# A two-layer vision tower on one core: exchanged operand roles in the tokenizer's products, and quantised input rows made three tiles ahead in the last feed-forward stage

## The reference, cut to what matters

```python
# tokenizer: x is [8, 256 features, 64 states, 2 (re, im)], all in fp32
dt = exp(log_dt);  A = -exp(inv_A_real) + 1j * A_imag;  dtA = A * dt[:, None]
dA = (1 + dtA / 2) / (1 - dtA / 2)
V = exp(log(dA)[:, :, None] * arange(256))            # powers 0..255
K = 2 * einsum('chn,hnl->chl', C * B, V).real         # tokens [8, 256, 256]
...
# last network, after a LayerNorm without gain or bias
def fp4_quant_dequant(x):          # blocks of 16 along the last axis
    scale = maximum(max(abs(xb)) / 6, 1e-12)
    return GRID[searchsorted(MID, abs(xb / scale))] * sign(xb) * scale
def fp4_linear(x, w): return quant(x) @ quant(w).T
h = h + fp4_linear(silu(fp4_linear(x, w_gate)) * fp4_linear(x, w_up), w_down)   # 256 -> 704 -> 256
```

## Time and profile before

| | us |
|---|---|
| median of three runs | 1653.43 (1650.32 to 1655.53) |
| the profiled execution | 1650.09 |
| span of its trace | 1648.4 |
| first product of the tokenizer to its last transpose | 55.9 to 117.6 |
| first gate product of the quantised stage to the end of the last residual sum | 1434.6 to 1646.6 |

### The profile page before, as it was taken

How to read it: one execution, slowest core, us unless ns; L and a number is a source line. 1 busy time by engine, 2 the same in 40 slices (tenths; PEclk the granted TensorE clock), 3 DMA queues, 4 the chain that set the end, 5 groups by cost and what they waited for, 6 DMA issues and landing times. The chain is left out here.

```text
span 1648.4 us, 24032 instructions
## 1 busy us (share of the span) xinstructions
PE 1312.1 (80%) x7107; PEld 1046.1 (63%) x7107; DVE 860.7 (52%) x2041; ACT 468.0 (28%) x1391; POOL 471.2 (29%) x660
## 2 busy tenths in 40 slices
PE   0688888616999705999989989999997899668787
PEld 0687766514777502577777767778877899445555
DVE  8746661311222251367767666675520377487774
ACT  1223330101222101354544543443200444111111
POOL 5731100152000162111211211111200577355564
PEclk9999996557999955599988997897575899789999
DMA  5006000122211130000000000000000300000000
GB/s 194 2 24 207 0 0 1 58 73 64 65 58 58 54 90 1 0 1 1 1 2 0 0 1 0 0 0 1 1 0 8 116 0 0 1 0 13 13 13 13
DMA packets 36440, 46.89 MB, mean 28 GB/s; under 512 B 4432, under 2 KB 32896, under 8 KB 36224
## 3 DMA queue, kind: packets, MB, share of 16 engines
q1 hardware_dynamic: 33152, 37.47, 7.0%
q0 software_dynamic: 3200, 8.43, 1.6%
HBM read 29.08 MB, written 16.80 MB: 28 GB/s over the span
## 5 line engine op out<-in xcount | busy, mean ns | idle before, releaser
L1997 PEld LDWEIGHTS fa_ps<-fa_v,fa_pt 128*128 128x128 f32 x1088 | 164.6, 226 | 3.3
L1997 PE MATMUL fa_ps<-fa_v,fa_pt 128*128 (+2 forms) x1088 | 165.8, 288 | 0.0
L1630 ACT ACTIVATE fa_e<-fa_ps,fa_nm 128x257 f32<-128x257 f32 x272 | 126.4, 473 | 97.7 <-DVE fa_nm L1808 96.7
L1516 POOL COPY fa_e<-fa_e 128x2 f32<-128x2 f32 x128 | 24.5, 192 | 398.1 <-ACT fa_e L1630 342.9
L1921 PE MATMUL fa_ps<-fa_xT,wf_qk 128*128 128x257 f32 (+1 forms) x320 | 111.0, 478 | 24.1 <-DVE fa_vc L1690 9.0
L1808 DVE TENSOR_REDUCE fa_nm<-fa_ps 128x2 f32<-128x514 f32 x136 | 93.7, 689 | 58.3 <-PE fa_ps L1949 46.6
L1284 PE MATMUL ex_ps<-we_raw,ex_xT 128*128 x320 | 118.4, 494 | 0.0
L446 PE MATMUL tk_ps<-tk_qb,tk_u 64*64 64x32 f32 x1024 | 54.8, 291 | 55.9 <-POOLq L312 55.9
L1976 PE MATMUL fa_ps<-ident,fa_e 128*128 128x128 f32 x512 | 95.6, 318 | 4.4 <-ACT fa_e L1630 4.0
L1921 PEld LDWEIGHTS fa_ps<-fa_xT,wf_qk 128*128 128x128 f32 (+1 forms) x320 | 60.8, 212 | 52.6 <-DVE fa_vc L1690 12.1
L1976 PEld LDWEIGHTS fa_ps<-ident,fa_e 128*128 128x128 f32 x512 | 69.1, 162 | 34.6 <-issue 18.9
(11 more groups left out here) (420 smaller groups left out, 2771.1 us busy)
## 6 DMA issues: line engine op xcount, KB each, us to landing
we_raw<-in_L_ffn_W SPq DMA_DIRECT2D x24, 384.0 KB, 8.7
x_rows<-tk_zero SPq DMA_DIRECT2D x1, 5120.0 KB, 18.9
ex_xin<-x_rows SPq DMA_DIRECT2D x40, 128.0 KB, 2.2
y_rows<-ex_y SPq DMA_DIRECT2D x40, 128.0 KB, 1.7
wq_raw<-in_ffn_rows SPq DMA_DIRECT2D x1, 2240.0 KB, 16.0
wg_f<-in_ff SPq DMA_DIRECT2D x2, 1024.0 KB, 8.6
out<-h SPq DMA_DIRECT2D x8, 256.0 KB
tk_c<-in_x SPq DMA_DIRECT2D x1, 1024.0 KB, 5.1
```

The costliest lines, as they stand in the source:

```text
L1630: last = cp(dst, ps[:, SB + 2 * par + t, 0:TOK], ACT.Exp, bias=nm[:, par, t:t + 1], accum_out=sums[:, p, sl, t:t + 1])
L1997: last = mm(dst, pt[:, par, c, t * P:(t + 1) * P], rhs, start=(c == 0), stop=(c == 1))
```

## The change

In the tokenizer's `products`, `QB` becomes the weights (64 rows by 32 columns) and `U` the moving operand (64 columns). The features of a block go in two halves (j), and a product writes partitions 32(2j + q) onward, so that four consecutive products have four different places in the array. `KT` is now indexed by (image, a) and half the features, and is turned by 128 ordinary products of 64 by 64 with the identity instead of 32 transposes. A bank then holds one image, and eight copies of 128 by 512 take the place of 16 of 128 by 256. On the host the features are laid out in another order (`mixed`).

In the quantised stage ScalarE makes the normalised rows (`centred`, with bias and scale), three tiles ahead; for that GpSimd makes one more vector at the start (`shift`, two operations), and ScalarE waits for it before its first copy. VectorE's `grid` takes the place of `scaled`: the correction is folded into the product (one step less), and the block maxima and reciprocals are kept in PSUM bank 0. VectorE quantises, and GpSimd rounds, the rows of tile u + 2 in body u; x and `xq` have two buffers. The turned rows share bank 6 with the turned hidden values, and ScalarE's last two hidden copies wait for the row transposes (`x_ps`). The weights' transposes use seven banks, so the eighth and ninth step wait for the first copies.

```diff
-                for i in range(HB):
+                for i in range(HB // 2):
                     for r in range(2):
-                        for q in range(2):
-                            rows = slice(q * NST, (q + 1) * NST)
-                            last = nc.tensor.matmul(ps[rows, p, i * NB:(i + 1) * NB], U[rows, p, r, i, :],
-                                                    QB[rows, p, r, i, :], start=(r == 0), stop=(r == 1))
+                        for j in range(2):
+                            for q in range(2):
+                                rows = slice(q * NST, (q + 1) * NST)
+                                outs = slice((2 * j + q) * NB, (2 * j + q + 1) * NB)
+                                last = nc.tensor.matmul(ps[outs, p, i * n:(i + 1) * n],
+                                                        QB[rows, p, r, j * HB // 2 + i, :],
+                                                        U[rows, p, r, j * HB // 2 + i, :],
+                                                        start=(r == 0), stop=(r == 1))
...
-            for g in range(8):
-                for j in range(4):
-                    last = nc.tensor.transpose(ps[:, g, j * P:(j + 1) * P], KT[:, 4 * g + j, :], ident[:, :])
+            for g in range(BATCH):
+                for a in range(NA):
+                    for j in range(2):
+                        half = slice(j * HH, (j + 1) * HH)
+                        last = nc.tensor.matmul(ps[half, g, a * 2 * NB:(a + 1) * 2 * NB], KT[half, g * NA + a, :],
+                                                ident[half, half], start=True, stop=True)
...
             def body(u, p):
-                s.base, s.n = s.before + 2 * ROUNDED * u, 0
-                if more(u):
-                    rows(u + 1, 1 - p)
+                s.base, s.n = s.before + 2 * ROUNDED * u - ROUNDED * without_rows(u), 0
+                if more(u, 2):
+                    rows(u + 2, p)
                 pool.wait_ge(z["hg_ready"], u + 1)
...
+            def centred(u, p):
+                if started(u, 2):
+                    act.wait_ge(z["xg_ready"], u - 1)
+                normalised(nc, mem, h, u, x[:, p, :]).then_inc(z["xn_ready"], 1)
+
+            act.wait_ge(z["norm_ready"], 1)
+            centred(0, 0)
+            centred(1, 1)
...
+                if turned is not None:
+                    act.wait_ge(z["x_ps"], turned)
                 cp(hT[:, 4, :], ps[:, TB + 1, 0:P], ACT.Copy)
...
+            def grid(src, t, m, top, sc, iv):
+                s(nc.vector.tensor_reduce(top, src, AX.X, ALU.max, apply_absolute_value=True))
+                s(ts(sc, top, 1.0 / 6.0, 1e-12, ALU.mult, ALU.max))
+                s(nc.vector.reciprocal(iv, sc))
+                s(nc.vector.scalar_tensor_tensor(t, src, 1.0 - 2.0 ** -24, bc(iv, 2, BLK), ALU.mult, ALU.mult))
+                s(ts(m.bitcast(I32), t.bitcast(I32), EXPO, None, ALU.bitwise_and))
+                s(ts(m, m, 1.0, SPREAD, ALU.max, ALU.mult))
...
-                if j == 8:
-                    pe.wait_ge(z["wt_act"], 1)
+                if j >= 7:
+                    pe.wait_ge(z["wt_dve" if j % 2 == 0 else "wt_act"], 1)
```

More of the change, by code:

```diff
@@ L424, in _ @@
                 dve.wait_ge(t_ps, g + 1)
[L425 to L430, removed]
+                nc.vector.tensor_copy(*placed(g)).then_inc(t_sb, 1)
+            dve.wait_ge(t_sb, BATCH)
         @block.tensor
@@ L2411, in tiles, with more, without_rows @@
             body(u, u)
-        with eng.Fori(1, TILES // 2) as i:
+        with eng.Fori(1, TILES // 2 - 1) as i:
             for p in range(2):
                 body(2 * i + p, p)
-        body(TILES - 1, 0)
+        for u in range(TILES - 3, TILES):
+            body(u, u % 2)
     def started(u, lag=1):
         return not isinstance(u, int) or u >= lag
-    def more(u):
-        return not isinstance(u, int) or u + 1 < TILES
+    def more(u, ahead=1):
+        return not isinstance(u, int) or u + ahead < TILES
+    def without_rows(u):
+        return max(u - (TILES - 2), 0) if isinstance(u, int) else 0
     def blocks(t):
@@ L2427, in turned_weights @@
     def turned_weights(j):
-        bank = ps[:, j % 8, :]
+        bank = ps[:, 1 + j % 7, :]
         if j < 6:
@@ L2476, in _ @@
             rows(0, 0)
+            rows(1, 1)
             s.begin()
@@ L2511, in body @@
                 if started(u, 2):
-                    hidden(u - 2)
+                    hidden(u - 2, u + 2 if more(u) else None)
                 if more(u):
                     rows(u + 1)
+                if more(u, 3):
+                    centred(u + 3, 1 - p)
             rows(0)
+            centred(2, 0)
             tiles(act, body)
-            hidden(TILES - 2)
-            hidden(TILES - 1)
+            hidden(TILES - 2, None)
+            hidden(TILES - 1, None)
         @block.vector
@@ L2543, in add @@
                 dve.sem_inc(z["h_done"], 1)
-            STEPS = 2 * (SCALED + 1) + 1
+            STEPS = 2 * GRID + 2
             def body(u, p):
                 s.base, s.n = s.before + (STEPS * u - 2 if started(u, 2) else (STEPS - 1) * u), 0
-                if more(u):
-                    if started(u):
-                        dve.wait_ge(z["xq_ready"], u)
-                    rows(u + 1, 1 - p)
+                s.base -= GRID * without_rows(u)
+                if more(u, 2):
+                    dve.wait_ge(z["xq_ready"], u + 1)
+                    rows(u + 2, p)
                 dve.wait_ge(z["up_ps"], u + 1)
@@ L2564, in body @@
                     add(u - 2)
-            dve.wait_ge(z["norm_ready"], 1)
             rows(0, 0)
+            rows(1, 1)
             s.begin()
             tiles(dve, body)
-            s.base, s.n = s.before + STEPS * TILES - 2 - (SCALED + 1), 0
+            s.base, s.n = s.before + STEPS * TILES - 2 - 2 * GRID, 0
             add(TILES - 2)
@@ L2602, in turn @@
                 for k in range(KC):
-                    last = nc.tensor.transpose(ps[:, XB, k * P:(k + 1) * P], xq[:, k * P:(k + 1) * P], ident[:, :])
+                    last = nc.tensor.transpose(ps[:, TB + 1, XC + k * P:XC + (k + 1) * P], xq[:, p, k * P:(k + 1) * P], ident[:, :])
                 last.then_inc(z["x_ps"], 1)
```

67 lines of the change are left out of this document (39 added, 28 removed).

## The result

The changed kernel takes **1582.56 us** (median of 4 runs, 1577.92 to 1586.19), the kernel before 1653.81 in the runs beside it (median of 4, 1650.32 to 1655.53): a ratio of 0.957 with a 95% interval of 0.954 to 0.960. The forecast was 1609, with a range of 1595 to 1629. One thing has to be known for all that follows: repeated runs of one and the same program differ, and with them the granted clock, so the kernel before took anything from 1632 us (mean clock 0.852) to 1671 us (0.826) in the later runs. I therefore compare stages inside the profiled executions, and medians only beside them.

A forecast was written before the change was run, and what follows sets the result against it. TensorE was taken to bound the tokenizer, a chain through four engines the quantised stage. Terms -17.4 + 8.0 + 1.5 - 7.7 - 27.6 = -43.2 gave 1606.9 (profiled) or 1610.2 (median), stated as 1609; range 1595 to 1629.

The forecast's parts named there:

- The sum: Whole kernel: all terms give -43.2 us, from the profiled 1650.1 to 1606.9, or 1610.2 from the median; stated 1609.
- Part 1: Tokenizer products: four array places work at once, so VectorE sets the pace at 4.8 us a block: -17.4 us.
- columns share the stream: Rival, chance 0.16: in the tokenizer, places with the same rows and other columns take turns: 1627 us.
- Part 2: Tokenizer, turning KT: 256 pairs at 53.5 ns, half clock, take 13.7 us against 5.66 now: +8.0 us.
- the clock comes up in the turning products: Rival, chance 0.22: the clock rises in the tokenizer's turning products, 6.8 us less: 1602 us.
- Part 3: Quantised stage's start: ScalarE waits for GpSimd's vector, so the first gate product comes later: +1.5 us.
- Part 4: Quantised stage's first tiles: rows are two tiles ahead, so 14.8 us instead of 22.5: -7.7 us.
- Part 5: Quantised stage's next 14 tiles: VectorE's mask and magic steps wait for GpSimd; 10.1 us a tile, not 12.07: -27.6 us.

The follow-up runs named there:

- two-place kernel: The changed kernel with the tokenizer's products run through column half j outermost, so at most two array places work at once: 1585.08 us.
- PSUM mask: The changed kernel with VectorE's mask step on the rows writing to PSUM, where the magic step reads it: 1575.82 us.

## Why the prediction was wrong

- **The sum, the step that failed.** It took every stage that the diff doesn't touch at nothing. The fused attention gave 20.5 us of the profiled 68.5, by the clock (0.82 for 0.79), with the place of a 0.22 us issue gap. My closing line named this as what would make the forecast wrong altogether, a stage that isn't touched and moves, but neither a rival nor the range allowed for it. Nor had I read anything from the medians of 1650 to 1656: three runs were too few to show that this kernel's time spreads over 39 us, and the 5 us that I called enough to tell a change don't hold here.
- **Part 1, products: right in its mechanism, and in its end partly by luck.** First to last start 55.9 to 93.1 us, 37.2 (37 to 40 forecast), and VectorE sets the pace. TensorE's products end at 93.4 where I had 93.2, but two errors cancel there: VectorE needed 5.1 us a block and not 4.8 and was done at 90.4 instead of 89.0, and TensorE's last block, partly at the higher clock, took 2.75 us and not 3.6. Four places at once held; the two-place kernel excludes *columns share the stream*. The granted clock was not fixed at the lower level, as I had assumed, but this hid behind VectorE.
- **Part 2, turning: mis-sized.** +8.0 forecast, +3.8 measured (9.43 us against 5.66 in the earlier trace rows); with the rest as forecast, this alone would have left the time inside the range. The price at half clock was right, and the clock didn't stay there. The windows of the kernel after, on either side of 98.5 us: 71 matmuls in 3.8 us at 0.50, 53.5 ns each, then 187 in 5.3 at 1.00, 28 ns each.

```profile
94.60:98.40 3.80, 3.79 (x71) 3.80 (x73) 0.69 (x1) 0.08 (x1) 0.00 (x0) 0.50 0.00 0
98.60:103.90 5.30, 5.30 (x187) 5.29 (x182) 2.07 (x3) 1.52 (x3) 0.00 (x0) 1.00 0.02 6
```

  The rival *the clock comes up in the turning products* (0.22) is what happened, for two thirds of its 6.8 us. My reason against it, that the products had never brought the clock up in 55 us, was about products in another order and with other gaps.
- **Part 3, the start: right.** From the first transpose to the first gate product 14.61 us (1386.64 to 1401.25), +1.25 against before, forecast +1.5.
- **Part 4, the first tiles: right.** 13.62 us for two tiles (1401.25 to 1414.87) in place of 22.54, -8.9 where I had -7.7: tile 1 needed 5.69 us, as forecast, and tile 0 only 7.93, since the clock came up a little sooner and turning cost less.
- **Part 5, the pace: right.** 141.2 us for 14 tiles (1414.87 to 1556.10) in place of 169.0, -27.8 where I had -27.6; 10.14 to 10.17 us a tile once settled, forecast 10.1. The PSUM mask shows that it was these two waits and that TensorE's own 9.55 (measured 9.68) lies right behind. One reading under it said too much: that in the kernel before the products keep their times beside GpSimd. The product of Silu and up does (0.89 us, one operand in PSUM), but none of the 34 product steps of line 2351, with both operands in SBUF, ran beside a GpSimd operation there. With one operand in PSUM that step doesn't wait (0.42 us), with both in SBUF it does (1.64). In the sum parts 4 and 5 leave out the tail, 1.5 us longer than before, where the last down product took 4.74 us at the lower clock and not 3.05.

So what the diff does to its own stages came to -47.6 us for a forecast of -43.2, most of the difference being part 2's clock: 1602.5 from the profiled 1650.1, inside the range. The other 20.5 are the attention's.

## What to carry to other kernels

Where the clock is granted and taken back inside a long stage, a few instructions more or fewer on one engine ahead of it (here four or eight on ScalarE) can move that stage by some 20 us. Time each stage by itself, in traces laid over each other from the stage's first matmul, and count a change's gain only in the stages it touches; shift the program by a few instructions that nobody needs before believing a gain or a loss elsewhere. And for VectorE steps beside GpSimd, one operand in PSUM is worth having on exactly those steps that wait: here 6.7 us from two of them.

## What the runs showed of the hardware

- A ScalarE issue gap of 0.22 us, whose place depends on how many ScalarE instructions stand ahead (four fewer, four more and eight more move it, one more doesn't), goes with 634 to 641 or 655 to 673 us in a stage of 3007 matmuls, in 15 traces of 16. The grants part company between 11 and 137 us behind it.
- Four products in four places of the array cost 28 ns a pair at the lower clock (3.64 us for 128) and 15.5 at the higher (1.99); two places 28 at the higher (3.58).
- A reciprocal on 16 numbers from SBUF to SBUF is not held up beside GpSimd (0.25 us); a product with two SBUF operands is (1.64 for 0.42), and so are one-operand steps on 256 columns (1.36 and 1.43 for 0.29).
